# A DRAM buffer between two transfers gets rows of 384 instead of 256 elements

## The reference

```python
x = x + _layernorm(_L0_attn_ref(_layernorm(x, axis=-1), WQ, WK, WV, WO), axis=-1)
x = x + _layernorm(_L0_ffn_ref(_layernorm(x, axis=-1), centroids, ln_g, ln_b, w1, b1, w2, b2), axis=-1)
```

## Time and profile before

| | |
|---|---|
| median of three runs | 404.59 us |
| the profiled execution's own time | 405.06 us |
| its span, first to last instruction | 403.3 us |
| TensorE busy, in that span | 316.1 us (78%) |
| VectorE busy | 333.7 us (83%) |
| ScalarE busy | 234.9 us (58%) |
| GpSimd busy | 239.9 us (59%) |
| packets of SP's DMA queue | 31888, 37.49 MB |

### The profile page before, as it was taken

One profiled execution on the slowest core, in us unless ns is written; L12 is line 12 of the kernel. 1 busy time (PEld: TensorE's weight loads), 2 busy tenths in 40 slices (PEclk: granted clock), 3 DMA queues, 4 the chain that ended last, 5 costly groups with the idle time before them and its releaser, 6 DMA issues.

```text
span 403.3 us, 10952 instructions
## 1 busy us (share of the span) xinstructions
PE 316.1 (78%) x3517; PEld 252.9 (63%) x3548; DVE 333.7 (83%) x1253; ACT 234.9 (58%) x574; POOL 239.9 (59%) x321
## 2 busy tenths in 40 slices
PE   2447879989999998999989988987105999998940
PEld 1325657766776776776667766754105999997930
DVE  7956798989899999799889988888661999998970
ACT  2201675675685685675765865556105898886940
POOL 4741373664675675665764765648540388887782
PEclk9998999999999999999999999999656999999995
DMA  7663674745735636636546546012035667666600
GB/s 209 117 115 36 114 167 62 124 109 66 133 75 78 113 79 81 110 66 93 97 78 89 99 82 107 25 35 68 21 95 172 183 190 195 181 190 174 182 31 6
DMA packets 34823, 42.82 MB, mean 106 GB/s; under 512 B 5481, under 2 KB 25197, under 8 KB 33232
## 3 DMA queue, kind: packets, MB, share of 16 engines
q1 hardware_dynamic: 31888, 37.49, 46.7%
q0 software_dynamic: 2304, 4.37, 3.4%
q10 hardware_dynamic: 576, 0.27, 0.3%
HBM read 30.65 MB, written 11.66 MB: 105 GB/s over the span
## 4 chain that ended last, share of the span: by engine, by line
PE 35%; POOL 20%; DMA 15%; DVE 13%; issue 12%; ACT 2%; SPq 1%; POOLq 1%; DVEq 0%; ACTq 0%
DMA aug<-nmT 11%; POOL out_x L546 9%; PE O L868 5%; POOL rsz L556 5%; PE S L834 5%; DVE nmf L1107 4%; PE ST L847 4%; PE S L829 3%; PE S L827 3%; PE MB L794 2%; PE O L872 2%; POOL xs_rows L479 2%; DMA aug<-qk_parts 2%; PE MB L882 2%; PE ST L856 2%
## 5 line engine op out<-in xcount | busy, mean ns | idle before, releaser
L1107 DVE TENSOR_REDUCE nmf<-S 128x2 f32<-128x512 f32 (+1 forms) x192 | 130.5, 683 | 25.0 <-PE S L834 14.2
L620 ACT ACTIVATE p<-ST 128x1024 f32<-128x1024 f32 x64 | 65.5, 1023 | 29.4 <-PE ST L847 29.2
L459 POOL TENSOR_SCALAR_AFFINE_SELECT p<-p 128x512 f32<-128x512 f32 x64 | 40.9, 639 | 51.4 <-ACT p L624 51.1
L455 POOL TENSOR_SCALAR_AFFINE_SELECT p<-p 128x512 f32<-128x512 f32 x64 | 40.8, 638 | 26.8 <-ACT p L620 26.4
L834 PE MATMUL S<-aug 126*128 126x128 bf16 x512 | 50.7, 222 | 0.0
L546 POOL DMA_INDIRECT out_x<-vaug,x_all x39 | 42.0, 1078 | 7.9 <-issue 7.9
L847 PE MATMUL ST<-aug 128*128 128x256 bf16 x256 | 38.6, 272 | 7.5 <-DMA aug<-nmT 6.6
L868 PE MATMUL O<-p,vaug 128*32 128x256 f32 x512 | 41.1, 390 | 2.5 <-POOL p L455 2.5
L834 PEld LDWEIGHTS S<-aug 126*128 126x128 bf16 x512 | 40.4, 99 | 3.5
L829 PE MATMUL S<-causal,identb 128*128 128x256 bf16 x128 | 36.0, 281 | 7.5 <-issue 4.5
L479 POOL DMA_INDIRECT xs_rows<-x_all,pos x32 | 32.8, 1026 | 10.9 <-issue 6.3
(11 more groups left out here) (162 smaller groups left out, 824.1 us busy)
## 6 DMA issues: line engine op xcount, KB each, us to landing
w1s<-in_w1x SPq DMA_DIRECT2D x39, 259.0 KB
qk_parts<-qkp SPq DMA_DIRECT2D x16, 384.0 KB, 2.8
aug<-qk_parts SPq DMA_DIRECT2D x32, 192.0 KB
aug<-qk_parts SPq DMA_DIRECT2D x32, 128.0 KB
x_all<-xs_rows SPq DMA_DIRECT2D x39, 67.0 KB
aug<-qk_parts SPq DMA_DIRECT2D x32, 64.0 KB
w_tab<-in_w2t SPq DMA_DIRECT2D x8, 256.0 KB
out_x<-vaug,x_all POOLq DMA_INDIRECT x39
```

The source lines that it names most:

```text
L455: g.affine_select(out=v, in_=v, compare_op=ALU.is_ge, fill=0.0, base=0, pattern=[[0, 4], [1, P]], channel_multiplier=-1).then_inc(s["sel0" ...
L459: g.affine_select(out=v, in_=v, compare_op=ALU.is_ge, fill=0.0, base=0, pattern=[[0, 4], [1, P]], channel_multiplier=-1).then_inc(s["sel1" ...
L620: a.activation(p0[:, gr % 2], ST0[:, :, :], ACT.Exp, scale=SCALE).then_inc(s["exp0"], 1)
L1107: v.tensor_reduce(dst, S[:, n % 2].rearrange("p (j n) -> p j n", j=k), op=ALU.max, axis=AX_X, negate=True).then_inc(s["red"], 1)
```

## The change

`qk_parts` gets rows of 384 elements in its last dimension, of which the first 256 are used through a view. A head's 512 bytes are then 768 bytes apart from the next head's, where they were 512 bytes apart and touched it. A feature's 16 heads, which were one piece of 8192 bytes in DRAM, are 16 pieces of 512 bytes; a feature's pitch goes from 8192 to 12288 bytes, a part's from 64 to 96 KB. Nothing else is edited.

```diff
--- before.py
+++ after.py
@@ -79,7 +79,7 @@
     SHIFT = P - 2
 
     xs_dram = nc.dram_tensor("xs_rows", (E * CAP + P, ROW), F32, kind="Internal").ap()
-    qk_dram = nc.dram_tensor("qk_parts", (RING, 2, 3, DH, NH, SEQ), BF16, kind="Internal").ap()
+    qk_dram = nc.dram_tensor("qk_parts", (RING, 2, 3, DH, NH, SEQ + P), BF16, kind="Internal").ap()[:, :, :, :, :, 0:SEQ]
 
     with ExitStack() as ctx:
         def sb(name, shape, dt=F32):
```

## The result

The changed kernel takes 411.49 us in the median of four runs (408.80 to 413.32), beside 404.72 for the kernel before in the same comparison: the ratio is 1.0149, with an interval of 1.0098 to 1.0200. It is slower by 1.5% by this ratio; the two medians are 6.8 us apart. 405.3 and no measurable change were forecast. Timed a second time, beside the runs of experiment 5, it gave 1.0139 (1.0087 to 1.0191). The profiled execution took 413.32 us, 1.8 above the median; its span is 411.6 us against 403.3.

The account below looks back on a forecast made before the run. No engine alone bounds the kernel; load phases ahead of the shift lie in the chain of waits. 0.1 us at the start plus 6 x 0.1 in waiting steps, +0.7 us, gave 405.3 us in the median; range 398.5 to 414.

Parts of the forecast that it names:

- rate of exchange: Attention loop: a load phase longer by d costs d in waiting steps, elsewhere only what exceeds the 0.6 us slack.
- slower rival: Tail of each load phase: small packets are paid although queues wait; 0.63 us a phase, 409.0 us; chance 0.30.
- the prediction's own sum: Growth d of a load phase counted once at the start, in six waiting steps, and beyond 0.6 us slack in six others.
- Seven load phases on the path: A sequence's six loads form a phase; the start's and six waiting steps' phases, before the shift, lie on the path.
- The sign of being wrong: A load phase changing by more than 0.2 us either way would make the forecast wrong.
- d = 0.1 us: Growth of each load phase from cutting, taken as the queue's own price at the phase's start.
- This hides the cutting: In the loads, a destination limit counting bytes, not packets, covers the cutting's price of 0 to 0.63 us a phase.
- The 48 ns of the small packets: Shift's packets beside the last loads; used for outer bounds: a load phase falls by 1.2 us or grows by 3.4.
- SP's issue costs nothing: On SP, cut loads issue as before, costed at nothing; even 0.1 us more each leaves 1.2 us before the shift.
- The store costs nothing: Store of the parts at the new pitch: bounded by 0 and 1.3 us, taken as 0; only the first store counts.
- The limit is at the destination: Loads are limited by SBUF partitions written: rates 218, 73, 52 GB/s as partitions go 24, 16, 8; 7.2 us a phase.
- Faster rival: Loads' source in DRAM: the 8192-byte pitch slows reads, the new one spreads them; 398.8 us at 1 us less; chance 0.25.

Follow-up runs that it names:

- experiment 5: Changed kernel again, 411.50 us; its pitch made 1280 bytes, 412.15, or 544, 411.60; kernel before with 24 satisfied waits ahead of each uncut load, 398.79.
- experiment 6: Kernel before with 15 satisfied waits ahead of each uncut load: 400.39 us; changed kernel with 12 waits ahead of each load: 403.25 and 404.38 us.
- Experiment 1: Kernel before with only K's three loads of each sequence cut, by gaps in SBUF, DRAM compact: 405.36 us, ratio 1.0026.
- Experiment 2: Changed kernel's DRAM layout and store, but each load reads 8192 bytes in one run, uncut, so results differ: 408.33 us, ratio 1.0073 to kernel before.

## Why the prediction was right or wrong

Its place, its rate of exchange and its range held; its size did not. It forecast 405.3 and no measurable change, and 411.5 came, within 398.5 to 414. That it lies within is no merit of the forecast's mechanism: the upper end was drawn for the slower rival, and two errors of opposite sign met. With the price of 2.0 us found in experiment 6 alone, the prediction's own sum would give some 22 us and 427.

- *Seven load phases on the path; what they grow by is paid in the waiting steps.* Right. The first phase grew by 1.09 us (10.70 to 11.79) and PE's wait there by 1.1. In the loop the phase grew by 0.84 us and the waits by 6.2 us, in 12 places instead of 7. With d = 0.84 the prediction's own sum, start + 6 d + 6 (d - 0.6), is 1.1 + 5.0 + 1.4 = 7.5 us; measured 7.3 in PE's waits. The sign of being wrong that the prediction set itself, a phase that changes by more than 0.2 us, came.
- *d = 0.1 us.* This term failed. It rested on "This hides the cutting": the engines spent 61 ns for 512 bytes where a packet alone needs 27.7, so a packet's own price was to vanish in the wait for the destination. The change's packets took 76 ns. Experiment 6 puts the price, pitch included, at 2.0 us a phase at the change's pace and 1.7 at a slower one. Experiment 1 shows that the cut has a price without the pitch: at its 3.72 us for the issues, uncut loads would have a phase near 10.0 (an estimate between 10.41 at 2.92 us and 9.71 at 4.14), and it had 11.11. My reading is that a queue works its packets in order, so that its waiting is not spare time in which the next packet's price could be paid; the runs show the price, not this mechanism of it. "Time to spare" was also read from a mean over 16 engines. The trace has a 4-byte packet at the end of each engine's part of a transfer, 76 in a step, which is 12 + 12 + 16 + 16 + 8 + 8 for the six loads and 2 for each of two shifts. So the loads of 24 and 8 partitions run on 12 and 8 engines. If the first eight take part in all six loads, each of them has 8 of the 96 packets, and 8 x 0.98 = 7.8 us is nearly the whole phase; which engine a packet ran on is not recorded, so this stays an estimate. The 48 ns of the small packets beside the loads were the row that warned, and I had it as a bound only.
- *SP's issue costs nothing.* Wrong as a number, 0.68 us instead of 0.37 for each load, and wrong in sign: 1.8 us more from first to last issue are worth 1.2 us of phase (10.88 to 9.71 with uncut loads, 2.37 to 4.14 us). So the net of 0.84 us is a price near 2.0 less a gain near 1.2, two terms that the forecast had as 0.1 and 0.
- *The store costs nothing.* Right, as far as the rows show. Its packets take 0.416 x 16 x 3.3 / 784 = 28.0 ns alone, 27.7 before, and the first one lands in 2.75 us as it did. In the loop it is not always far from its reader, though: in two of the later steps of each trace the loads start only when it has landed, after 4.3 us before and 4.5 and 4.7 after. These two and the first store are the chain's 3% of `qk_parts<-qkp`.
- *The limit is at the destination.* Not refuted and not shown. Changing the order, so that neighbours write other partitions, took 5 us off, which fits it. But the falling rates that it was read from depend on the windows: the earlier trace rows leave out 140.6:141.1, and the last window runs past the loads. Three windows of 2.4 us from 135.65 on have 188, 48 and 92 GB/s (by the starts of the packets), where the prediction's equal parts of 2.4 us would be 164, 109 and 55. And the number of engines at work changes with the partitions, 12, 16 and 8, which no run keeps apart from them. Where the prediction went on to "a limit at the destination counts bytes, not packets", no row bore it. A slip without weight: 27.7 ns for 512 bytes allow 296 GB/s, not 282.
- *Faster rival, the pitch relieves the source.* Out: four pitches with cut loads and one without, none faster than before. Whether the pitch adds a part of its own is open. Experiment 2 allows it (phase +0.2 us, the time clear of none), and so does 1024 against the others (phase 0.1 to 0.3 us less).
- *Slower rival.* Its outcome came: small packets are paid, and the shift behind them lands later. Its place, the tail of each phase, is not borne out by the last part's 64 GB/s, and its reason, queues that work in order, was not tested. It was priced at 0.63 us and 409.0, and given 0.30.

That experiment 1 seemed to show no cost has the same reason: with K alone cut, issues take 3.72 us, a pace that is worth about 1 us of phase, and half of the price is 1 us. The two nearly cancel, where +0.23 us and +0.3%, not clear of none, were measured. This accounting is worked out afterwards from the other runs, not tested by one of its own. Why experiment 2 is slower, with no cut at all, stays open.

## What to carry to other kernels

Engine time that looks like waiting did not cover the price of more packets here. When a transfer is cut into pieces, expect a cost for each piece even where the engines seem to have time to spare in the mean, and take the price from small packets in the same crowd, not from small packets alone. If a wait stands behind a burst of transfers, look at the burst itself: try an order in which neighbours write different partitions, and do not take a faster issue for a better one. A measured change can be the difference of two larger terms, so vary the pace and the pieces apart.

## What the runs showed of the hardware that was not expected

- Six loads of 768 KB, 8192 bytes a partition, on partitions 0 to 47, end sooner if they are issued more slowly: with the six issues in 2.37, 2.92, 4.14 and 5.98 us the shift behind them lands 10.88, 10.41, 9.71 and 8.96 us after the first issue. The kernel follows: 404.7, 401.4, 400.4 and 398.8 us. Why they slow each other is not shown.
- The issue of a load of 24, 16 or 8 partitions with 16 runs of 512 bytes each takes 0.59 to 0.80 us on SP in the loop, one with a single run of 8192 bytes 0.29 to 0.42. A store of 128 partitions with 6 runs each takes 0.38 and so is no guide to it. It happens with the gap on either side, DRAM or SBUF.
- Loads of 512-byte packets on 24, 16 and 8 partitions hold the engines 76 ns for a packet when they follow each other; the same bytes in 8192-byte packets 61 ns for 512 bytes. The 512-byte packets of the store, from 128 partitions and alone, take 28 ns.
- A load of 24 partitions ends in 12 semaphore increments of its engines, one of 16 in 16 and one of 8 in 8; the shift, on two partitions, in 2.
